# Two attentions of a megakernel: transposes, query/key instructions and evictions in a new order within each pair of tiles, and a part of GpSimd's halving given to VectorE

## The reference

```
layer 0 (linear attention)            layer 1 (retention)
q, k = elu(x Wq)+1, elu(x Wk)+1       q, k = rotate(x Wq), rotate(x Wk);  v = x Wv
S_t = S_(t-1) + k_t v_t^T             out_s = sum over t <= s of
z_t = z_(t-1) + k_t                           (q_s . k_t) decay^(s-t) v_t / sqrt(8)
y_t = q_t S_t / (q_t . z_t + eps)     y = groupnorm(out) per head of 8 channels
x = x + gate * (y Wproj)              x = x + gate * ((silu(x Wg) * y) Wo)
```

## Time and profile before

| | |
|---|---|
| median of 3 runs (lowest, highest) | 1056.55 us (1055.17, 1057.34) |
| the profiled execution, its own time | 1054.64 us |
| its span, first to last instruction | 1052.8 us |
| busy PE, DVE, ACT, POOL | 860.5, 829.7, 609.6, 711.0 us |
| first attention: first halving to last residual | 61.3 to 315.4 us |
| second attention: the same | 415.5 to 686.4 us |
| clock of PE granted, mean | 0.928 of full |

### The profile page before, as it was taken

How to read it: one execution, slowest core, us unless ns; L and a number is a source line. 1 busy time by engine, 2 the same in 40 slices (tenths; PEclk the granted TensorE clock), 3 DMA queues, 4 the chain that set the end, 5 groups by cost and what they waited for, 6 DMA issues and landing times. The chain is left out here.

```text
span 1052.8 us, 24355 instructions
## 1 busy us (share of the span) xinstructions
PE 860.5 (82%) x5240; PEld 622.6 (59%) x5240; DVE 829.7 (79%) x2581; ACT 609.6 (58%) x1524; POOL 711.0 (68%) x450
## 2 busy tenths in 40 slices
PE   5699999999968977888898988639888731999993
PEld 5456666666645754555555655426656521999993
DVE  5468888888875994888888888767988770899995
ACT  2545555555427965565656566347765212999992
POOL 4478878878853535999999999645599562255554
PEclk9799999999987998999999999859999855999997
DMA  8520000000000000000000000064566654544420
GB/s 243 165 66 2 0 0 0 0 0 0 0 1 5 0 1 1 11 11 20 10 20 10 20 10 20 21 184 109 149 207 208 192 193 143 159 131 134 133 68 20
DMA packets 64934, 70.11 MB, mean 67 GB/s; under 512 B 8965, under 2 KB 52178, under 8 KB 64740
## 3 DMA queue, kind: packets, MB, share of 16 engines
q1 hardware_dynamic: 50612, 47.20, 16.2%
q0 software_dynamic: 6368, 16.89, 4.7%
q10 hardware_dynamic: 7872, 5.08, 1.7%
HBM read 32.32 MB, written 24.50 MB: 54 GB/s over the span
## 5 line engine op out<-in xcount | busy, mean ns | idle before, releaser
L475 POOL TENSOR_TENSOR a_kv<-a_qk,a_vv 128x2304 f32<-128x2304 f32 (+1 forms) x64 | 252.0, 3938 | 37.1 <-DVE a_qk L446 32.6
L485 PE MATMUL a_pS<-a_kv,utri 128*128 128x360 f32 (+3 forms) x768 | 259.7, 475 | 10.7 <-POOL a_kv L475 10.7
L574 DVE TENSOR_TENSOR a_tt<-a_pS,a_qk 128x360 f32<-128x360 f32 (+3 forms) x384 | 201.5, 527 | 75.4 <-PE a_pS L485 75.2
L485 PEld LDWEIGHTS a_pS<-a_kv,utri 128*128 128x128 f32 x768 | 140.5, 191 | 96.2 <-issue 29.8
L591 POOL TENSOR_TENSOR a_tt<-a_tt 128x1152 f32<-128x1152 f32 (+1 forms) x64 | 144.7, 2260 | 37.7 <-DVE a_tt L574 37.6
L2016 POOL DMA_INDIRECT out_dram<-x_o,x_place x71 | 69.1, 974 | 76.1 <-DVE x_o L2003 75.1
L602 DVE TENSOR_REDUCE a_nd<-a_tt 128x144 f32<-128x720 f32 (+3 forms) x128 | 104.3, 817 | 1.0 <-POOL a_tt L591 0.9
L538 ACT ACTIVATE a_tt<-a_pI 128x144 f32<-128x144 f32 (+1 forms) x96 | 39.8, 415 | 96.0 <-PE a_pI L493 95.9
L1596 POOL DMA_INDIRECT ys<-m_S,m_dest x64 | 63.0, 984 | 35.2 <-issue 12.7
L546 ACT ACTIVATE a_qT<-a_pQ 128x128 f32<-128x128 f32 x96 | 26.5, 276 | 98.9 <-PE a_pQ L410 83.3
L1954 PE MATMUL x_pZ<-w,x_hT 128*128 x568 | 75.9, 277 | 1.4 <-issue 1.4
(11 more groups left out here) (299 smaller groups left out, 2103.4 us busy)
## 6 DMA issues: line engine op xcount, KB each, us to landing
x_yl<-ys SPq DMA_DIRECT2D x71, 193.5 KB, 2.4
X<-xs SPq DMA_DIRECT2D x16, 256.0 KB, 5.3
kx<-m_kc SPq DMA_DIRECT2D x64, 64.0 KB
ax<-m_pc SPq DMA_DIRECT2D x64, 64.0 KB
m_S<-X SPq DMA_DIRECT2D x16, 256.0 KB, 3.6
xs<-X SPq DMA_DIRECT2D x15, 256.0 KB
w<-in_L_ffn_W_dram SPq DMA_DIRECT2D x1, 2048.0 KB
m_S<-gw ACTq DMA_DIRECT2D x6, 256.0 KB, 2.9
```

The source lines that it names most:

```text
L475: pool.tensor_tensor(kv[:, t:t + 2, :, :, :].rearrange("p t h j i -> p (t h) j i"), kk.unsqueeze(2).to_broadcast([P, 2 * H, J, D]), rows.u ...
L485: pe.matmul(pS[c][:, 0:(h1 - h0) * SC], K.utri[:, :], flat[:, h0 * SC:h1 * SC], start=True, stop=True).then_inc(u_done, 1)
L574: v.tensor_tensor(tt[:, t, h0:h1, :, 0:D], pS[c][:, 0:(h1 - h0) * SC].rearrange("p (h j i) -> p h j i", i=D, j=J), q[:, h0:h1, :].unsqueez ...
```

## The change

In both layers:

- The transposed q leaves the QKV bank pQ for pI, which now holds the inter-tile product, one transposed q and the transposed y. QKV matmuls and VectorE's reading of pQ no longer stand in its way; in their place it waits until ScalarE has emptied pI.
- PE's order: QKV of the first tile directly after the state sum, then the projection, then the y and q transposes; at the step's end QKV, x transposes, y, q. In layer 0 y is transposed and evicted a tile at a time, in layer 1 both tiles at the step's end.
- ScalarE: QKV evictions and q's eviction move ahead of `act_normalise` in both halves of the step, y's second eviction and the gate go to the end.
- VectorE: `vec_qk` of the next batch's even tile stands before the second tile's products, and the residual behind `vec_state`.
- GpSimd, layer 1: `pool_gate` handles the pair three steps back instead of two, and stands between the halving and the rotation sum.

In layer 1 alone GpSimd halves 12 of the 16 heads; VectorE sums these in one instruction and the other four, over all eight products (and the ninth column), in a second.

```diff
+    HH, SUMS = (H, 1) if layer == 0 else (12, 2)
-        YT = H * J
-        QT = 3 * P
+        QT = H * J
+        YT = QT + P
...
         def pe_transpose_q(pe, b, t):
-            pe.wait_ge(v_ready, m)
             pe.wait_ge(qk_ready, qk_count(b, t))
-            pe.wait_ge(qk_free, m)
+            wait(pe, inter_ready, 3 * b + t - 1)
             wait(pe, qT_ready, 3 * b + t - 1)
-            pe.transpose(pQ[:, QT:QT + P], qk[:, 0, t, :], K.ident[:, :]).then_inc(q_T, 1)
+            wait(pe, yT_read, y_issued(b, t - 1))
+            pe.transpose(pI[:, QT:QT + P], qk[:, 0, t, :], K.ident[:, :]).then_inc(q_T, 1)
+        def evacuated(pe, b, t):
+            wait(pe, inter_ready, min(3 * b + t, 3 * B) if isinstance(b, int) else 3 * b + t)
+            wait(pe, qT_ready, min(3 * b + t, 3 * B) if isinstance(b, int) else 3 * b + t)
+            wait(pe, yT_read, y_issued(b, t))
+        def pe_transpose_y(pe, at, b, t):
+            pe.wait_ge(y_ready, 2 * at[0] + at[1] + 1)
+            evacuated(pe, b, t)
...
         def act_qT(act, b, t):
             act.wait_ge(q_T, 3 * b + t)
-            if known(b, 1):
-                act.wait_ge(qkv_ps, 4 * b + 4 + t)
             wait(act, inter_ps, 3 * b + t - 1)
...
         def pool_halve(pool, b, u):
-            two = lambda i: tt[:, t:t + 2, :, :, i:i + D // 2].rearrange("p t h j i -> p (t h j) i")
+            two = lambda i: tt[:, t:t + 2, 0:HH, :, i:i + D // 2].rearrange("p t h j i -> p t (h j) i")
         def vec_sum(v, b, t):
-            v.tensor_reduce(nd[:, t % 2, :, :], tt[:, t, :, :, D // 2:rows], AX.X, ALU.add).then_inc(red_done, 1)
+            v.tensor_reduce(nd[:, t % 2, 0:HH, :], tt[:, t, 0:HH, :, D // 2:rows], AX.X, ALU.add).then_inc(red_done, 1)
+            if HH < H:
+                v.tensor_reduce(nd[:, t % 2, HH:H, :], tt[:, t, HH:H, :, 0:rows], AX.X, ALU.add).then_inc(red_done, 1)
...
         def pe_step(pe, b, u, first=False):
-            if cur and not first:
-                pe_states(pe, b, ta)
-            if out:
-                pe_project(pe, *out)
             if cur:
+                if not first:
+                    pe_states(pe, b, ta)
                 if ta > 0:
                     pe_inter(pe, b, ta)
                 pe_state_sum(pe, b, ta)
-                pe_transpose_q(pe, b, ta + 1)
                 if known(b, 1):
                     pe_qkv(pe, b + 1, ta)
-            if back:
-                pe_transpose_y(pe, back, b, u)
+            if out:
+                pe_project(pe, *out)
+            if cur and layer == 1 and u == 0 and known(b, 1):
+                pe_gate(pe, b + 1)
+            if back and layer == 0:
+                pe_transpose_y(pe, back, b, ta)
             if cur:
-                if layer == 1 and u == 0 and known(b, 1):
-                    pe_gate(pe, b + 1)
+                pe_transpose_q(pe, b, ta + 1)
                 pe_states(pe, b, tb)
                 pe_inter(pe, b, tb)
                 if tb < 3:
                     pe_state_sum(pe, b, tb)
-                    pe_transpose_q(pe, b, tb + 1)
                 if known(b, 1):
                     pe_qkv(pe, b + 1, tb)
                 if u == 1 and known(b, 2):
                     pe_transpose_x(pe, b + 2)
+            if back:
+                pe_transpose_y(pe, back, b, tb)
+            if cur and tb < 3:
+                pe_transpose_q(pe, b, tb + 1)
         def act_step(act, b, u, phase, more=True):
                 if ta > 0:
                     act_inter(act, b, ta)
-                if more:
-                    act_normalise(act, b + 2, ta)
-                act_qT(act, b, ta + 1)
                 if known(b, 1):
                     act_qkv(act, b + 1, ta)
-            if back:
-                act_yT(act, *back)
+                act_qT(act, b, ta + 1)
+            if back and layer == 0:
+                act_yT(act, *back, 0)
+            if more:
+                act_normalise(act, b + 2, ta)
             if layer == 1 and last:
                 act_square(act, *last)
             if cur:
                 act_inter(act, b, tb)
-                if more:
-                    act_normalise(act, b + 2, tb)
             if layer == 1 and last:
                 act_sd(act, *last)
             if cur:
+                if known(b, 1):
+                    act_qkv(act, b + 1, tb)
                 if tb < 3:
                     act_qT(act, b, tb + 1)
-                if known(b, 1):
-                    act_qkv(act, b + 1, tb)
-                if layer == 1 and u == 0 and known(b, 1):
-                    act_gate(act, b + 1, (phase + 1) % 3)
+            if more:
+                act_normalise(act, b + 2, tb)
+            if back:
+                act_yT(act, *back, 1)
+            if cur and layer == 1 and u == 0 and known(b, 1):
+                act_gate(act, b + 1, (phase + 1) % 3)
         def vec_step(v, b, u):
-            if out:
-                vec_residual(v, *out)
             if cur:
                 vec_product(v, b, ta, 2)
             if last:
                 vec_sum(v, last[0], 2 * last[1])
             if cur:
                 vec_state(v, b, ta)
+            if out:
+                vec_residual(v, *out)
             if last:
                 vec_sum(v, last[0], 2 * last[1] + 1)
+            if cur and known(b, 1):
+                vec_qk(v, b + 1, ta)
             if cur:
                 vec_product(v, b, tb, 0)
...
                 vec_product(v, b, tb, 1)
-                if known(b, 1):
-                    vec_qk(v, b + 1, ta)
...
         def pool_step(pool, b, u, phase):
             if last:
                 pool_halve(pool, *last)
+            if layer == 1 and out:
+                pool_gate(pool, *out, (phase + (u - 3) // 2) % 3)
             if ahead:
                 if layer == 1:
                     pool_rope(pool, *ahead)
                 pool_kv(pool, *ahead)
-            if layer == 1 and back:
-                pool_gate(pool, *back, (phase - 1) % 3)
```

More of the change, by code:

```diff
@@ L408, in pe_qkv @@
                 wait(pe, qk_free, m)
-                wait(pe, qT_ready, 3 * b - 3 + t)
             pe.matmul(bank_of(b, t, start)[:, 0:3 * P], hT[:, t * P:(t + 1) * P], wqkv, start=True, stop=True).then_inc(qkv_ps, 1)
@@ L486, in pe_states, with y_issued @@
                           start=True, stop=True).then_inc(u_done, 1)
+        def y_issued(b, t):
+            return 4 * b + t - 4 if layer == 0 else 2 * b + t // 2 - 2
         def pe_inter(pe, b, t):
@@ L491, in pe_inter @@
             pe.wait_ge(r_ready, 3 * b + t)
-            wait(pe, yT_read, 2 * b + t // 2 - (1 if t % 2 else 2))
+            wait(pe, yT_read, y_issued(b, t))
             pe.matmul(pI[:, 0:H * J], qT[:, :], R[:, :, :].rearrange("p h j -> p (h j)"),
@@ L503, in pe_transpose_q @@
         def pe_transpose_q(pe, b, t):
-            m = 4 * b + 4 + t - 1
-            if isinstance(b, int):
-                m = min(m, NT)
-            pe.wait_ge(v_ready, m)
             pe.wait_ge(qk_ready, qk_count(b, t))
-            pe.wait_ge(qk_free, m)
+            wait(pe, inter_ready, 3 * b + t - 1)
             wait(pe, qT_ready, 3 * b + t - 1)
-            pe.transpose(pQ[:, QT:QT + P], qk[:, 0, t, :], K.ident[:, :]).then_inc(q_T, 1)
[L514 to L522, removed]
+            wait(pe, yT_read, y_issued(b, t - 1))
[3 more added lines that the diff above has]
+            wait(pe, qT_ready, min(3 * b + t, 3 * B) if isinstance(b, int) else 3 * b + t)
+            wait(pe, yT_read, y_issued(b, t))
+        def pe_transpose_y(pe, at, b, t):
+            pe.wait_ge(y_ready, 2 * at[0] + at[1] + 1)
+            evacuated(pe, b, t)
+            if layer == 0:
+                pe.transpose(pI[:, YT:YT + P], y[:, t % 2, :], K.ident[:, :]).then_inc(y_T, 1)
+            else:
+                pe.transpose(pI[:, YT:YT + P], y[:, 0, :], K.ident[:, :])
+                pe.transpose(pI[:, YT + P:YT + 2 * P], y[:, 1, :], K.ident[:, :]).then_inc(y_T, 1)
         def pe_project(pe, b, u):
             n = 2 * b + u
-            pe.wait_ge(yT_ready, n + 1)
+            pe.wait_ge(yT_ready, 2 * n + 2 if layer == 0 else n + 1)
             wait(pe, x_done, n)
@@ L536, in act_inter @@
             act.wait_ge(inter_ps, 3 * b + t)
-            wait(act, red_done, n - 3)
+            wait(act, red_done, SUMS * (n - 3))
             act.activation(tt[:, t, :, :, D], pI[:, 0:H * J].rearrange("p (h j) -> p h j", h=H),
@@ L571, in vec_product @@
             q = qk[:, 0, t, :].rearrange("p (h i) -> p h i", h=H)
-            wait(v, red_done, n - 3)
+            wait(v, red_done, SUMS * (n - 3))
             v.wait_ge(u_done, 3 * n + c + 1)
@@ L611, in act_square @@
             n = 2 * b + u
-            act.wait_ge(red_done, 2 * n + 2)
+            act.wait_ge(red_done, SUMS * (2 * n + 2))
             wait(act, var_done, n)
@@ L642, in vec_y @@
             v.wait_ge(rec_done, n + 1)
-            wait(v, y_T, n)
+            wait(v, y_T, 2 * n if layer == 0 else n)
```

(12 more changed lines are left out.)

11 lines of the change are left out of this document (6 added, 5 removed).

## The result

| | before | after |
|---|---|---|
| median (lowest, highest) | 1056.30 us (1055.17, 1057.34) | 1072.61 us (1069.46, 1074.70) |
| ratio, 95% interval | | 1.0152 [1.0124, 1.0180] |
| profiled execution, own time; its span | 1054.64; 1052.8 us | 1069.46; 1067.7 us |
| first attention, first to last halving | 61.31 to 306.55: 245.24 us | 60.83 to 318.20: 257.37 us |
| second attention, the same | 415.49 to 676.03: 260.54 us | 425.75 to 690.73: 264.98 us |

The change makes the kernel slower by 16.3 us, where 6.6 were forecast. In the profiled executions the span grows by 14.9 us: 12.1 come from the first attention and 4.4 from the second, 16.6 together before rounding; what lies outside these two stretches gives back 1.7. So the two attentions alone account for the 16.3 us of the medians.

The account below looks back on a forecast made before the run. No engine is full; a loop through several engines sets the pace. 7.7 - 0.8 (first attention) + 0.7 - 1.0 (second) = +6.6 us, so 1061.2 profiled and 1063 for the median; range 1050 to 1075.

Parts of the forecast that it names:

- The sign: Whole kernel: the change makes it slower, +6.6 us; slower was given 0.58.
- the stall: First attention: one PE stall of about 1.4 us, for ScalarE's normalisation, replaces two of about half a microsecond.
- First attention, first pair: PE waits for the late query/key instruction until S + 2.69; the half takes 7.50 us, gaining 0.50.
- the walk: PE's new order stepped through with start-to-start times from the rows; first-attention batch 16.56 us, taken as +0.55.
- First attention, second pair: Normalisation behind three QKV evictions delays the last x transpose; next states at 9.06 us, 1.06 more than half a batch.
- the lower bound: First-attention batch: ScalarE's instructions overlap by 0.1 each and waits end 0.1 sooner; 16.3 us, +0.3.
- The upper bound: First-attention batch: shared-bank waits show as 0.30 us gaps at two places, +0.6 more, so +1.2.
- 14 x 0.55 = +7.7: First attention, batches 0 to 13, which have a batch after next: +7.7 us (4.2 to 17).
- Second attention: Batch 16.9 to 17.3 us against 17.04, set by ScalarE and PE; +0.05 x 14 = +0.7 (-2.8 to +4.2).
- Head division: Second attention: halving falls to 1.65 us, VectorE's sums become 0.645 + 0.445; both hidden by waits.
- Faster: GpSimd alone paces the second attention: -16 us, about 1047; with first attention's normalisation also in time, 1032. Chance 0.22.
- Slower by the shared bank: Shared-bank evictions only half hidden at two transposes a batch; each attention loses 13 us, 1090. Chance 0.03.

Follow-up runs that it names:

- Experiment 6: Changed kernel with PE's loop over batches unrolled by two in both attentions; 1068.52 us, ratio 1.0110.
- experiment 9: Kernel before with only PE's loop of both attentions unrolled to two batches an iteration; 1054.50 us, ratio 0.9996.
- experiment 3: Kernel before with only the second attention's head division added (GpSimd halves 12 heads, VectorE sums the other four directly); 1055.50 us, ratio 1.0006.
- experiment 4: Changed kernel with GpSimd halving all 16 heads in both attentions; 1073.25 us, ratio 1.0159.
- experiment 8: Changed kernel with ScalarE's odd-tile normalisation back ahead of the QKV evictions and GpSimd halving all 16 heads; 1039.93 us, ratio 0.9840.
- experiment 1: Changed kernel with ScalarE's odd-tile normalisation moved back ahead of the QKV evictions; 1038.40 us, ratio 0.9828.
- experiment 2: Changed kernel with the y transposes ahead of the x transposes at the step's end; 1066.90 us, ratio 1.0094.
- experiment 10: Changed kernel with the odd-tile normalisation back ahead of the QKV evictions and PE's loop unrolled to four batches an iteration; 1029.59 us, ratio 0.9763.
- experiment 11: Changed kernel with the odd-tile normalisation back ahead of the QKV evictions and y transposes ahead of x transposes; 1040.70 us, ratio 0.9859.

## Why the prediction was right or wrong

The sign and the stall held; the size was 6.6 against 16.3 us. The step that failed is the stretch between the last x transpose and the next states, in both attentions, where the edge of PE's loop was put at nothing.

*First attention, first pair.* Forecast 7.50, measured 7.66. The late query/key instruction lets QKV go 2.74 after the states (2.69 forecast) as said. The excess is at the second q transpose, 0.25 behind y and 0.21 ahead of the states (160.43, 160.68, 160.89), where the walk had 0.11 each.

*First attention, second pair.* Forecast 9.06, measured 9.40: here lies the failed step. PE stood for the normalisation as described, and the transpose came even earlier than forecast (8.59 against 8.84 after the pair's states, ScalarE's instructions overlapping as in the lower bound). But from it to the next states the walk had 0.22, and it took 0.81. "I take the walk itself, +0.55, as most short matmuls in the rows follow each other without such a gap" was the wrong choice between the bounds: the measured +1.07 a batch (17.07 against 16.00) stands near the upper one, +1.2, which had 0.6 for such gaps. Experiment 6 says what most of it is: 0.4 from the edge of PE's loop, which the prediction has nowhere and which the kernel before doesn't show (experiment 9). The upper bound had the gaps from another cause, the waits on the shared bank, so that its size comes close is luck. So the term "14 x 0.55 = +7.7" measured 11 x 1.07 between batches inside the loop, and 0.7 to 0.9 at batches before and behind it: 12.1 for the whole attention, with the gain of the last batch taken off.

*Second attention.* Forecast +0.05 a batch, measured +0.44 to +0.48. The gate starts 9.16 after the states (forecast 9.1 to 9.3), the fourth tile's states at 13.00 (12.8 to 13.2); from there it takes 4.48 where 4.1 were forecast, and the difference is again the gap at the edge, 0.51 behind the last y transpose. Experiment 6 brings every other batch to 17.1, which is the forecast.

*The sum.* For the first attention it had 7.7 - 0.8 = +6.9 and measured +12.1, for the second 0.7 - 1.0 = -0.3 and measured +4.4: short by 5.2 and 4.7. The 11 edges of each loop at 0.4 make 4.4, so the edge accounts for most of both, while the other errors of the first attention (+0.3 a batch at short transposes, -0.25 at ScalarE) nearly cancel.

*Head division.* The halving at 1.65 and the sums at 0.645 and 0.445 were right to 1%, and that dividing the heads gains nothing was shown three times (experiments 3, 4 and 8).

*The rivals.* Faster: its condition, ScalarE's gate at 8.4 or earlier, wasn't met (9.16); GpSimd doesn't set the pace, as experiment 8 shows. The other half of that rival, the normalisation in time, is the one with the money in it: experiment 1 does that and gains 18 us over the kernel before, 6.3 in the first attention and 10.7 in the second. Slower by the shared bank (1090): QKV and the state sum hide the evictions at the other transposes, and experiment 1, which keeps the shared bank, is faster than the kernel before; no run puts q back into its old bank, so what sharing costs by itself stays open. The rule behind it, to rotate groups through banks (the Trainium skill, Perfetto Trace Analysis, section Optimizing Tensor Performance), is borne out at one place: the third q transpose, now in the bank of the inter product, waits 12.5 us in ten batches for that bank's eviction, where the y transposes waited 8.2 before. That is 0.4 us a batch more, far from the 1090 that the prediction worked out from it.

*What would show it.* VectorE's wait for the states was to grow once a batch; it fell to 0.80, because the wait moved one instruction up, to its y (1.46), which waits until PE has transposed the y before it. That wait was overlooked and is off the path (experiment 2). At the other pair, where the wait was to nearly vanish, it fell from 0.70 to 0.38 (161.91).

## What to carry to other kernels

An instruction moved behind others on an in-order engine is priced by who reads it next: one normalisation of 0.48 us, put behind three evictions, stopped TensorE for 1.15 us every batch of the first attention and 0.47 of the second, and turned a reordering worth -18 us into +16. When an engine has no work queued at the end of a loop's body, count the loop's edge as an instruction of its own, and unroll before tuning further (here some 7 us, from a ratio of 0.9828 in experiment 1 to 0.9763 in experiment 10). Work taken off a busy engine that waits for others at that place (0.48 us a pair here) comes back as waiting.

## What the runs showed of the hardware

- The edge of a TensorE loop took 0.4 us (0.64 against 0.22 us from the last transpose to the next matmul), in both attentions, with a stall of TensorE ahead of it (the changed kernel) or without (experiments 1 and 11); in the kernel before it took nothing that the time shows. The compare-and-branch of TensorE's sequencer took 0.208 us of it (median of 24 rows in the changed kernel), and 0.076 where a loop ended; the register instructions beside it fill the rest (experiment 6). The Trainium skill (Advanced Engine Details and Errata, section Control Flow Timing) gives about 0.05 us for an unconditional branch and 0.11 us for a conditional one. For the branch back to the loop's start the trace has nearly twice the latter, and the trace decides.
- The profile names it "issue" in one kernel and a VectorE product that had ended 0.34 us earlier in another (experiment 1, 163.41): the idle time before it, not the releaser, is what to read.
- GpSimd's halving took 2.12 to 2.16 us for 1024 elements and 1.64 to 1.67 for 768, in the kernels before and after and in experiments 1, 3, 4, 8 and 9.
